# A GNN kernel's sorting stage: code rows by DRAM broadcast, selections on ScalarE, steps of six tiles

## The reference, cut to what matters

```
src, dst: (412500,) int32, dst ascending;  edge_attr_16: (412500, 16);  edge_type_8: (412500,)
x = layernorm(x + gated_update(x, sum over edges into a node of A[edge_type] @ x[src]))
x = layernorm(x + conv(x, sum over edges of (x[src] outer edge_attr) @ We))
x = layernorm(x + two relational layers, mean over edges per type, with W[edge_type])
x = layernorm(x + sheaf layer, messages to both ends of each edge)
```

## Time and profile before

| | us |
|---|---|
| measured, median of 3 runs | 15,686.25 (15,683.95 to 15,699.72) |
| span of the profiled execution | 19,204.3 |
| sort in it, from POOL's first to its last scatter | about 304 to 8,933 |
| POOL busy, whole span | 8,212.6 |
| DVE busy, whole span | 12,447.3 |

### The profile page before, as it was taken

How to read it: one execution, slowest core, us unless ns; L and a number is a source line. 1 busy time by engine, 2 the same in 40 slices (tenths; PEclk the granted TensorE clock), 3 DMA queues, 4 the chain that set the end, 5 groups by cost and what they waited for, 6 DMA issues and landing times. The chain is left out here.

```text
span 19204.3 us, 476192 instructions
## 1 busy us (share of the span) xinstructions
PE 11642.0 (61%) x158466; PEld 9132.4 (48%) x158467; DVE 12447.3 (65%) x22949; ACT 7744.0 (40%) x17320; POOL 8212.6 (43%) x8491
## 2 busy tenths in 40 slices
PE   1223232232222322223887999979978699999998
PEld 0112121121111211112665888866656488888887
DVE  3334344353443434434887888878878799999998
ACT  1122122131221312213665666656656455555554
POOL 2443434434334343344993111159989611111111
PEclk9855555555555555555998999999999899999999
DMA  7112111121111211113774222248777522323322
GB/s 186 41 40 68 43 53 54 41 67 43 54 54 41 67 43 54 54 42 94 220 220 125 104 109 104 108 144 225 224 196 225 149 83 85 84 84 84 84 84 72
DMA packets 1742522, 1898.15 MB, mean 99 GB/s; under 512 B 1011017, under 2 KB 1449883, under 8 KB 1716987
## 3 DMA queue, kind: packets, MB, share of 16 engines
q1 hardware_dynamic: 1617117, 1853.32, 32.5%
q0 software_dynamic: 123008, 41.82, 1.4%
q10 hardware_dynamic: 2078, 0.15, 0.0%
HBM read 1445.12 MB, written 449.46 MB: 99 GB/s over the span
## 5 line engine op out<-in xcount | busy, mean ns | idle before, releaser
L633 POOL DMA_INDIRECT rec<-sort_ring,sort_idx x3712 | 3662.5, 987 | 5267.2 <-issue 4334.9
L1280 DVE TENSOR_TENSOR e_full<-e_feats,e_masks 128x1280 bf16<-128x1280 bf16 x3537 | 2789.0, 849 | 243.1 <-ACT e_feats L1237 209.9
L712 PE MATMUL sort_ps_count<-sort_hot,upper_b 128*128 x500 | 255.3, 511 | 3904.5 <-DVE sort_hot L790 3405.9
L681 ACT CAST sort_rows_dst<-sort_ps_rows 128x512 f16<-128x512 f32 x980 | 533.2, 586 | 4688.0 <-PE sort_ps_rows L750 3268.1
L1180 PE MATMUL e_acc<-e_full,e_sel 128*128 128x384 bf16 (+1 forms) x11760 | 2117.7, 327 | 355.4 <-DVE e_full L1280 355.4
L750 PE MATMUL sort_ps_rows<-ident_h,sort_code 128*128 128x128 f16 x7840 | 1079.4, 308 | 1993.8 <-DVE sort_code L867 884.2
L837 DVE TENSOR_TENSOR sort_over<-sort_ps_late,sort_late_base 128x16 f32<-128x16 f32 x225 | 39.3, 175 | 2910.5 <-remote 2809.0
L712 PEld LDWEIGHTS sort_ps_count<-sort_hot,upper_b 128*128 128x128 bf16 x500 | 52.0, 104 | 3935.5 <-issue 3931.7
L1432 PE MATMUL e_acc<-e_outer,e_sel 128*128 128x272 f32 x7840 | 1895.3, 397 | 3.9 <-DVE e_outer L1527 3.9
L750 PEld LDWEIGHTS sort_ps_rows<-ident_h,sort_code 128*128 128x128 f16 x7840 | 683.5, 132 | 2385.3 <-issue 1638.1
L1235 ACT CAST e_masks<-e_kind 128x1280 bf16<-128x1280 fp8e4 x1179 | 1482.6, 1258 | 773.4 <-DVE e_full L1280 734.2
(11 more groups left out here) (452 smaller groups left out, 27178.9 us busy)
## 6 DMA issues: line engine op xcount, KB each, us to landing
e_hot<-stream SPq DMA_DIRECT2D x888, 480.0 KB, 3.7
stream<-sort_made SPq DMA_DIRECT2D x98, 2568.0 KB, 7.6
e_sel<-stream SPq DMA_DIRECT2D x1176, 160.0 KB, 2.4
e_st<-stream SPq DMA_DIRECT2D x99, 1888.0 KB, 7.3
sheaf_gather<-stream SPq DMA_DIRECT2D x393, 384.0 KB, 3.1
e_hot<-stream SPq DMA_DIRECT2D x294, 448.0 KB, 3.5
tail<-sort_made SPq DMA_DIRECT2D x98, 660.0 KB, 9.4
sheaf_by_dst<-tail SPq DMA_DIRECT2D x491, 128.0 KB, 3.0
```

The costliest lines, as they stand in the source:

```text
L633: nc.gpsimd.indirect_dma_start(out=rec[q], out_offset=bass.IndirectOffsetOnAxis(ap=idx[:, s, q, c:c + 1], axis=0), in_=ring[:, s, q, c, :] ...
L1280: last = v.tensor_tensor(full[q & 1][:, :, 0:cols].rearrange("p j (t k f) -> p j t k f", t=TYPES, k=3)[:, :, :, k, :], feats[q & 1][:, :, ...
```

## The change

- `C` is 6: 6 steps in a quad, 150 in all, rounded up to 152, each with 24 indirect DMAs.
- POOL waits once for four DMAs (`landed[c & 1]`, two semaphores in turn) instead of before each. `scattered` is given at the second tile of a step.
- DVE's one-hots `hot` have a ring of four, and `find`, PE's `count` and ACT's keys run three steps ahead (`AHEAD`). PE sums per group alone (12 products of 160 columns); the ranks inside a step's tiles come from comparing each key with the others of its row on DVE (`same`, `earlier`, `within`).
- The numbers of late edges are added one step later (`number_late`), for the last step of a quad only after the first build that follows.
- All four blocks' records are loaded at once. DVE transposes the codes (`read_codes`), SP writes them to a small DRAM table `scr` with four DMAs a block, and reads them back spread over 128 partitions (`spread_dst`, `spread_codes`). PE has no part in the builds.
- `sel` is made on ScalarE (`select`): 40 times Abs(code - iota), five times Relu(1 - that).
- Fields are int16 instead of f32, and one buffer (`own48`) is allocated after the sort.

```diff
-C = 4
+C = 6
+AHEAD = 3
+HOT_RING = 4
...
 def load_attrs(n):
...
-                        sp.wait_ge(scattered, i + 1)
+                        sp.wait_ge(scattered, i + 1 + SLACK)
...
+                def keep_codes(b, q):
+                    sp.wait_ge(codes_made, b + 1)
...
+                    for k in range(4):
+                        at = slice(32 * k, 32 * k + 32)
+                        sp.dma_start(scr[q][:, at].rearrange("(k r) s -> r k s", r=32),
+                                     codes_t[at, q, :].rearrange("r (k s) -> r k s", s=32)).then_inc(scr_in[q], 16)
+                def spread_dst(n, b, q):
...
+                    sp.wait_ge(sel_t_made, b + 1)
...
+                    sp.dma_start(rows_dst[:, :, :], scr[q][0:NT, :].partition_broadcast(P)).then_inc(dst_in, 16)
+                def spread_codes(b, q):
+                    for w in range(3):
+                        sp.wait_ge(codes_used, b * 3 + w + 1)
...
+                        sp.dma_start(rows_code[:, js, :], scr[q][NT + js.start:NT + js.stop, :].partition_broadcast(P))\
+                            .then_inc(code_in[w], 16)
...
                 def move_blocks(n, blocks):
...
-                    load_records(n * Q, n, 0)
-                    load_records(n * Q + 1, n, 1)
                     for q in range(blocks):
-                        store(n * Q + q, q & 1)
-                        if q + 2 < blocks:
-                            load_records(n * Q + q + 2, n, q + 2)
+                        load_records(n, q)
+                    for q in range(blocks):
+                        keep_codes(n * Q + q, q)
+                    for q in range(blocks):
+                        spread_dst(n, n * Q + q, q)
+                        spread_codes(n * Q + q, q)
+                        if q > 0:
+                            store(n * Q + q - 1, (q - 1) & 1)
+                    store(n * Q + blocks - 1, (blocks - 1) & 1)
...
                         for c in range(C):
+                            pool.wait_ge(landed[c & 1], u * (16 * Q * C // 2) + (s * C // 2 + c // 2) * (16 * Q))
+                            if c == 1:
+                                pool.sem_inc(scattered, 1)
...
                             for q in range(Q):
-                                pool.wait_ge(landed[q], u * (16 * C) + (s * C + c) * 16)
-                                pool.sem_inc(passed, 1)
                                 nc.gpsimd.indirect_dma_start(
...
+                def select(b, q, h):
...
+                        for j in range(SEL_CHUNK):
+                            at = k * SEL_CHUNK + j
+                            last = nc.scalar.activation(apart[:, k & 1, j, :], m.iota[:, :], ACT.Abs,
+                                                        bias=codes[:, q, at:at + 1], scale=-1.0)
...
+                        nc.scalar.activation(sel[:, k * SEL_CHUNK:(k + 1) * SEL_CHUNK, :], apart[:, k & 1, :, :],
+                                                    ACT.Relu, bias=m.iota[:, 1:2], scale=-1.0, saturate=False)\
...
+                    for c in range(C):
+                        mm(ps_off[:, hot_of(a), :].squeeze(1), m.upper_b[:, :], one(c), start=c == 0, stop=c == C - 1)
+                    for c in range(C):
+                        last = mm(ps_total[:, hot_of(a), :].squeeze(1), m.ones_b[:, :], one(c), start=c == 0, stop=c == C - 1)
...
+                    with dve.Fori(i0 + 1, i1) as i:
+                        find(i + AHEAD)
+                        rank_keys(i)
+                        count_within(i + AHEAD)
+                        number_late(i)
+                        place(i)
...
                 with dve.Fori(0, QUADS - 1) as n:
-                    one_quad(n + 1)
+                    i1 = one_quad(n + 1)
                     for q in range(Q):
-                        build(n * Q + q, q & 1)
+                        read_codes(n, n * Q + q, q)
+                    build(n * Q, 0, 0)
+                    number_late(i1)
+                    for q in range(1, Q):
+                        build(n * Q + q, q, q & 1)
```

More of the change, by code:

```diff
@@ L69 @@
 EVEN = "the count is even, and the loop goes by twos"
+SIXTH = 1366
+assert all((n >> 1) * SIXTH >> 12 == n // C for n in range(TILES + C))
 BOUNDED = "a block's range ends with the last tile, and a step or two of pads follow"
@@ L890, in build @@
[L890 to L893 removed]
+                            last = v.tensor_scalar(hot3[:, js, k, :], rows_code[:, js, 0:P], m.code_of[:, k:k + 1], None, ALU.is_equal,
+                                                   saturate=False)
```

548 lines of the change are left out of this document (291 added, 257 removed).

## The result

The changed kernel takes **15,895 us** (median of 4 runs, 15,885 to 15,950) beside 15,693 for the kernel before (4 runs, 15,684 to 15,747). The ratio is 1.0129, 95% interval 1.0107 to 1.0151. The forecast was 15,310 us, 2.4% faster.

The account below looks back on a forecast made before the run. The chain through the builds was taken to bound the sort, then POOL after the change: 24 periods of 186 us, a last quad, set-up and tail make 4,735 against 5,111, 376 less: 15,310 us, range 15,000 to 15,720.

Parts of the forecast that it names:

- the price of POOL in the sum: Sort: each scatter costs POOL 1.29 us, 186 us a quad; any other pace would show the prediction wrong.
- the part on a build: Builds on DVE: PE and ACT's 6.6 us go, DVE's 23.7 stay; four builds take 95 us.
- The lock quoted in the prediction: Beside builds: two-port DVE operations shut GpSimd out, up to 1.9 us longer per DMA; not seen, so not charged.
- The chain through the builds decides, by 13 us over POOL: Sort before the change: waits through the builds set the period, about 199 us against POOL's 186.
- 9 unexplained us a period: Sort before: the chain's check gave 190 us a quad, but 5,111 us in all left about 9 more each.
- Rival B: Sort: POOL already bound the measured runs at 1.38 us a DMA; only pads go, 88 us, 15,600; chance 0.13.
- the 376 us: Sort: the total gain forecast, from 5,111 us to 4,735.
- the 83 for pads: POOL in the sort: 64 pad DMAs go, saving 83 us at 1.29 each.
- the 3,518 us above the median: Profiled span over the measured 15,686 us: all put on the sort, making it about 5,111 us when measured.
- a term that the prediction set aside: Sort: POOL's idle 137 us a quad in the profile, times 24, were said to be not there to win.
- A: POOL's 0.30 us gap belongs to the wait: 1.07 us a DMA, 677 us less, 15,010; chance 0.12.
- D: Builds: broadcasts from DRAM are slow, 50 us a block, 17,600; sign: DVE waits for rows; chance 0.11.

Follow-up runs that it names:

- k2: Changed kernel with its code rows 128 columns wide instead of 130, on a prompt-signal chip: 15,720 us, 1.0004 of the kernel before.
- h1: Changed kernel plus short stages ahead of the sort, timing scatters beside round trips or DVE operations, late-signal chip: round trip 0.65 us alone, 2.80 beside scatters.
- k1: Kernel before, unchanged, profiled again on a prompt-signal chip: 15,714 us.
- f1: Kernel before, unchanged, profiled again on a late-signal chip: 19,135 us.
- f2: Changed kernel, unchanged, on a late-signal chip: 16,334 us, 0.8517 of the kernel before.
- e3: Changed kernel with each broadcast cut to its first row, on a late-signal chip: 16,326 us, 0.8473 of the kernel before.
- h2: Changed kernel plus other short stages ahead of the sort (scatter pitch, size and kind varied), prompt-signal chip: round trip 0.65 us in all eight.

## Why the prediction was wrong

**The step that failed** is the price of POOL in the sum, 1.29 us a scatter. The prediction named "if POOL's pace with eight DMAs under way is not 1.29" as a sign of being wrong, and it was 5,341/3,648 = 1.46. The price of 1.29 covers 4,706 us. Of the 636 above it, 337 are stretching beside comparisons, 88 more stretching beside the steps (161, less the 73 that 1.29 holds), and 211 idle time.

The 337 come from the part on a build: DVE's 23.7 us stay, with 16.77 for the comparisons, and "these operations show none of it, and the sum holds with 1.29". The row was read rightly, but for another operation. The source was 1,664 columns in one piece, and the changed kernel reads it as 13 rows of 128 with a pitch of 130. In the diff of `rows_code` and `spread_codes` this stood as `PITCH`. Each comparison now takes 1.14 us instead of 1.94 (1.06 instead of 1.86 from one to the next of the nine), and a scatter that starts among them takes 0.83 us longer, 0.70 on average over the 480 that meet one: 337 us in this trace (k2, h1). The Trainium skill says which form is fast (VectorE: DVE Perf Modes, "What auto-detection actually checks": one SBUF source and an SBUF destination whose outermost dimensions are both even or equal); 1,664 against 13 is neither, 13 against 13 is. `sel_t`, whose destination is one piece of 4,992 against 39 rows, stayed at 5.41 us, as that sentence has it. The lock quoted in the prediction (SBUF — State Buffer) is then what the trace shows, 1.80 us for 0.97.

By k2 this is the smaller part of the miss. Between 15,310 and 15,895 lie 585 us, and the flat row gives back 175; with it the kernel still takes 15,720, as the kernel before does.

**The bound of the kernel before** is the larger part. "The chain through the builds decides, by 13 us over POOL" was argued from 9 unexplained us a period. k1 shows POOL alone: above 1.27 us a scatter its sort has 365 us of idle time, 306 of it ended by landings, and 79 of stretching. So the 321 us between 5,111 and POOL's 4,790, which the change was to win, were mostly POOL's own, and a build that starts earlier or lasts shorter wins none of them. Rival B had this pace: its 1.38 us a scatter is 5,158/3,712 = 1.39. Of the 376 us, the 83 for pads came (81 by k1's price), and of idle time 154 that no term had. The account closes at 15,714 - 81 - 154 + 334 + 85 = 15,898. That is a sum over what was measured, and no forecast: B itself said 15,600, and neither it nor another rival had the stretching.

**The profiler.** That the 3,518 us above the median lay in the sort was right (k1: 5,158 us against the 5,111 derived). That they were the profiler's doing was wrong: f1 runs as slowly untraced. So a term that the prediction set aside is real on late chips. There each of a build's first round trips between PE and ACT takes 5 to 11 us until POOL has run dry. From f1, ACT, then POOL:

```profile
4116.62 0.58 ACT L681 CAST sort_rows_dst<-sort_ps_rows 128x512 f16<-128x512 f32 x1 [5.02 <-remote]
4125.03 0.58 ACT L681 CAST sort_rows_dst<-sort_ps_rows 128x512 f16<-128x512 f32 x1 [7.83 <-remote]
4136.23 0.58 ACT L681 CAST sort_rows_dst<-sort_ps_rows 128x512 f16<-128x512 f32 x1 [10.62 <-remote]
4143.12 1.07 ACT L681 CAST sort_rows_dst<-sort_ps_rows 128x512 f16<-128x512 f32 x2 [0.21 <-PE sort_ps_rows L750]
...
4136.36 0.97 POOL L633 DMA_INDIRECT rec<-sort_ring,sort_idx  x1 [0.30 <-issue]
4273.50 1.04 POOL L633 DMA_INDIRECT rec<-sort_ring,sort_idx  x1 [136.17 <-issue]
```

At 4,143 POOL has stopped and a trip costs nothing. All four builds (4 x 30.3, and 15 to the next scatter) lie in POOL's 136 us. The changed kernel has no such trips in its builds and loses most of this: POOL's idle time above 0.303 falls from 3,783 us in f1 to 689 in f2. That is its 15% there, as the change in these traces shows it; which part of the change brings how much was not separated.

**What held.** POOL's idle time before a quad's first scatter is under 10 us. The gap stays at 0.30, so a wait fewer is worth nothing by itself (against A). The first broadcast of a quad is issued at 3068.47 and its reader starts at 3075.49, 7 us against 6 assumed. In all DVE waits 281 us for such rows (48 times, 11.3 at most), which the prediction had named as a sign of D, but the bytes cost next to nothing (e3). An Abs of 128 columns has 387 ns. DVE does not wait for late sums. Apart from the gap, all of this lay beside POOL.

**What was in no term.** Waits were priced by the 0.30 us alone. Their other price, the landing itself, is 306 us before and 110 after. Two groups under way give a scatter 5.1 us to land. In the changed kernel's trace its last packet ends a median of 0.80 us behind the issuing instruction, but one in twenty takes over 6 us, and the longest 7.4. That these are late because of the bulk transfers beside them is my reading; no run on a prompt chip took those away.

## What to carry to other kernels

Before a DVE operation is called unchanged, look at the shape of both of its operands, not at its line: padding that was put there for another reason can switch its mode, and where GpSimd issues DMAs the faster mode is paid by GpSimd. Where one engine has no long gap, sum its own instructions at their undisturbed duration first, then its stretching and its short waits. Only what is left over can belong to a chain. And when a profiled span differs from the measured time by a fifth, run the kernel again beside it before the difference is put down to the profiler.

## What the runs showed of the hardware

- On three chips, register and semaphore instructions of 0.6 to 0.8 us stood beside GpSimd's scatters, and signals between engines were late; on the others not. Measured by itself on one chip of each kind, beside scatters every 1.27 us, a round trip PE, ACT, PE was 2.80 or 0.65 us. The scatters' own landing had the same median in both, 0.8 us behind the end of the issuing instruction. Beside scatters that comparisons stretched to a pitch of 2.11 us even the late chip was prompt. What it is on the chip stays open.
- An operation with two SBUF inputs of 960 f32 columns stretches a scatter as much (1.83 us, h1) as the fast comparison does (1.80).
- A scatter of 64 rows has a pitch of 1.21 us against 1.27 for 128; a direct DMA of the same bytes from GpSimd 0.53 us (h2). One more GpSimd operation of 8, 48 or 128 columns ahead of each scatter makes a pitch of 1.49, 1.60 and 1.80 us.
- In the changed kernel and in k2 every 112th scatter had idle time of its own ahead of it, 83 and 57 us in all, with no semaphore to wait for. What it is stays open.
